# A recommender tower in 32 blocks per tile: other places for the parts, the portions and the last tile's MLP

## The reference

```python
e = stack([tbl_f[ids[:, f]] for f in range(32)], axis=1)        # (1024, 32, 64)
p, q = e[:, ROW_IDX], e[:, COL_IDX]                             # i and j of each of 496 pairs
z = einsum('bne,hne,bnh->bn', p, kernel, q)                     # kernel: (64, 496, 64)
h = concatenate([z, dense_ctx], axis=1)                         # (1024, 512)
h = maximum(h @ W_top1 + b_top1, 0)
h = maximum(h @ W_top2 + b_top2, 0)
y = h @ W_top3
```

## Time and profile before

| | |
|---|---|
| median of 3 runs | 755.47 us |
| the profiled execution | 754.49 us |
| its span, first to last instruction | 752.7 us |
| TensorE matmuls busy | 437.4 us, 58% of the span |
| VectorE busy | 361.6 us, 48% |
| ScalarE busy | 340.9 us, 45% |
| GpSimd busy | 241.9 us, 32% |
| granted TensorE clock, mean | 0.853 of 2.4 GHz |

### The profile page before, as it was taken

How to read it: one execution, slowest core, us unless ns; L and a number is a source line. 1 busy time by engine, 2 the same in 40 slices (tenths; PEclk the granted TensorE clock), 3 DMA queues, 4 the chain that set the end, 5 groups by cost and what they waited for, 6 DMA issues and landing times.

```text
span 752.7 us, 15352 instructions
## 1 busy us (share of the span) xinstructions
PE 437.4 (58%) x5552; PEld 320.8 (43%) x5552; DVE 361.6 (48%) x476; ACT 340.9 (45%) x2897; POOL 241.9 (32%) x260
## 2 busy tenths in 40 slices
PE   1001002588219971399614995159941599999896
PEld 1001001465007750168402783027820478777685
DVE  0010010697007870088601885028940388989881
ACT  0110000485226852267412774128641385986872
POOL 6777773003750047400573006720077100000000
PEclk9999999699559995599855998559975699999999
DMA  4663110000100001000010001100011000000000
GB/s 119 217 201 108 26 27 16 1 3 13 26 19 2 2 17 26 16 1 3 19 26 13 2 3 22 26 9 2 3 24 27 6 2 2 3 2 3 2 4 1
DMA packets 14571, 19.65 MB, mean 26 GB/s; under 512 B 7192, under 2 KB 7840, under 8 KB 14496
## 3 DMA queue, kind: packets, MB, share of 16 engines
q0 software_dynamic: 8192, 8.40, 5.6%
q1 hardware_dynamic: 6304, 10.27, 4.3%
HBM read 18.65 MB, written 0.00 MB: 25 GB/s over the span
## 4 chain that ended last, share of the span: by engine, by line
PE 42%; issue 36%; DVE 10%; ACT 5%; another core or an unknown queue 5%; POOL 1%; DMA 1%; DVEq 0%
PE side_ps L468 13%; PE u_ps L448 12%; PE u_ps L455 10%; DVE prod_s L383 6%; ACT prod_s L293 5%; PE side_ps L498 4%; DVE h L393 1%; DVE emb_t L357 1%; DVE prod_t L370 1%; POOL emb L252 1%; PE u_ps L433 1%; PE side_ps L514 1%; ACT h_t L320 1%; PE side_ps L490 1%
## 5 line engine op out<-in xcount | busy, mean ns | idle before, releaser
L293 ACT ACTIVATE prod_s<-prod_s 128x64 f32<-128x64 f32 x1408 | 300.2, 320 | 318.2 <-DVE prod_s L383 189.0
L252 POOL DMA_INDIRECT emb<-tbl,ids_sb x256 | 241.7, 944 | 344.2 <-DVE prod_s L383 265.7
L293 ACT ACTIVATION_READ_ACCUMULATOR prod_s<-prod_s 128x1 f32 x1408 | 267.7, 233 | 81.9 <-issue 81.8
L370 DVE TENSOR_TENSOR prod_t<-u_ps,emb_t 128x1024 f32<-128x1024 f32 x128 | 155.8, 1217 | 254.7 <-PE u_ps L448 211.7
L383 DVE TENSOR_TENSOR prod_s<-u_ps,emb 128x640 f32<-128x640 f32 (+4 forms) x192 | 158.4, 860 | 86.0 <-remote 40.5
L455 PE MATMUL u_ps<-k_sb,emb_t 64*128 64x512 f32 (+4 forms) x768 | 147.0, 495 | 88.0 <-issue 62.5
L468 PE MATMUL side_ps<-prod_t,pick_sb 128*32 128x128 f32 x2048 | 103.0, 284 | 162.4 <-issue 161.4
L448 PE MATMUL u_ps<-emb_t,k_sb 64*128 64x128 f32 x2048 | 146.8, 287 | 41.0 <-issue 34.1
L448 PEld LDWEIGHTS u_ps<-emb_t,k_sb 64*128 64x128 f32 x2048 | 134.1, 196 | 77.0 <-issue 54.4
L468 PEld LDWEIGHTS side_ps<-prod_t,pick_sb 128*32 128x32 f32 x2048 | 67.2, 112 | 194.5 <-issue 191.2
L455 PEld LDWEIGHTS u_ps<-k_sb,emb_t 64*128 64x128 f32 x768 | 62.8, 198 | 110.3 <-issue 71.4
(11 more groups left out here) (12 smaller groups left out, 22.6 us busy)
## 6 DMA issues: line engine op xcount, KB each, us to landing
k_sb<-k_pairs SPq DMA_DIRECT2D x16, 512.0 KB
emb<-tbl,ids_sb POOLq DMA_INDIRECT x256
w_sb<-w SPq DMA_DIRECT2D x1, 1024.0 KB
w_sb<-w SPq DMA_DIRECT2D x1, 512.0 KB
h<-dense SPq DMA_DIRECT2D x8, 8.0 KB
out<-y_row SPq DMA_DIRECT2D x8, 0.5 KB
ids_sb<-ids SPq DMA_DIRECT2D x1, 112.0 KB, 2.4
id_sb<-ident SPq DMA_DIRECT2D x1, 64.0 KB, 2.4
```

The source lines that it names most:

```text
L252: nc.gpsimd.indirect_dma_start(emb[t % EMBS][:, f * EMBED:(f + 1) * EMBED], None, tables[f], bass.IndirectOffsetOnAxis(ap=ids_sb[:, t, f:f ...
L293: last = nc.scalar.activation(slot, slot, ACT.Copy, accum_out=acc_ps[:, t % 2, column:column + 1])
L370: last = nc.vector.tensor_tensor(prod_t[at % TRING][:].rearrange("p (h x) -> p h x", h=HALVES), u, low.unsqueeze(1).to_broadcast([P, HALVE ...
```

## The change

Five things. (1) In the last group of blocks the ragged block y moves from the end to place 28, and the kinds of the blocks 26 to 31 go from T S T T T S to S T S T T T; numbers of each kind stay. (2) Parts 1 and 2 are turned behind blocks 5 and 13. (3) The portions stand behind blocks 5, 9, 13, 18, 23, 27 and 31. Where a portion and a part share a block, the portion comes first, as it did in the code before. (4) In the last tile, the third portion of picks stays behind block 29. (5) The last tile's rest is rewritten. The first layer's units go to the slots of blocks 29 and 30, the second's to that of block 31, one bank for each group of 128 units, with chunk 0 of the inputs first, before the last picks are there; the straight sums are transposed into the unused half of `acc_ps`; the relus alternate between ScalarE and VectorE, each with a semaphore. Elsewhere only names change (`last` becomes `done` or `stop`).

```diff
-    order = ["SS", "TSSTSS", "TSTTSTSTSS", "TSTTSTSTTSTTTS"]
+    order = ["SS", "TSSTSS", "TSTTSTSTSS", "TSTTSTSTSTSTTT"]
...
-        blocks += zip([*fulls[:2 * a], x, *fulls[2 * a:], y], [kind == "T" for kind in order[a]], strict=True)
+        group = [*fulls[:2 * a], x, *fulls[2 * a:], y]
+        if a == GROUPS - 1:
+            group = [*fulls[:2 * a], x, *fulls[2 * a:3 * a], y, *fulls[3 * a:]]
+        blocks += zip(group, [kind == "T" for kind in order[a]], strict=True)
...
-TURN_AT = {6: 1, 15: 2}
+TURN_AT = {5: 1, 13: 2}
...
-LATE_SPREAD_AT, HIDDEN1_AT, LATE_HIDDEN1_AT, HIDDEN2_AT, SUMS_AT, LATE_SUMS_AT, SPREAD_AT = 4, 8, 12, 17, 21, 25, 29
+LATE_SPREAD_AT, HIDDEN1_AT, LATE_HIDDEN1_AT, HIDDEN2_AT, SUMS_AT, LATE_SUMS_AT, SPREAD_AT = 5, 9, 13, 18, 23, 27, 31
+LAST_SPREAD_AT = 29
...
+        last = TILES - 1
+        h1_ps = [u_ps[SLOT_USE["u", last, n] % USLOTS][:, half * BANK:half * BANK + P]
+                 for n in (NB - 3, NB - 2) for half in range(2)]
+        h2_ps = [u_ps[SLOT_USE["u", last, NB - 1] % USLOTS][:, half * BANK:half * BANK + P] for half in range(2)]
+        spread_ps = acc_ps[:, (last + 1) % 2].rearrange("p (c b) -> p c b", c=S_CHUNKS)
...
# ScalarE
-            copy_acc(TILES - 1)
-            copy_spread(TILES - 1)
-            hidden1(TILES - 1)
-            hidden2(TILES - 1)
-            copy_logit(TILES - 1)
+            copy_acc(last)
+            act.wait_ge(last_turned, 1)
+            nc.scalar.activation(h0_t[:, T_CHUNKS:], spread_ps, ACT.Copy).then_inc(last_copied, 1)
+            act.wait_ge(picked, TILES * NT)
+            nc.scalar.activation(h0_t[:, 1], side_ps[:, 0], ACT.Copy).then_inc(last_copied, 1)
+            for m in (0, 2):
+                act.wait_ge(last_h1_mm, m + 1)
+                nc.scalar.activation(h1_t[:, m], h1_ps[m], ACT.Relu, bias=b1_sb[:, m:m + 1]).then_inc(last_h1_a, 1)
+            act.wait_ge(last_h2_mm, 1)
+            nc.scalar.activation(h2_t[:, 0], h2_ps[0], ACT.Relu, bias=b2_sb[:, 0:1]).then_inc(last_h2_a, 1)
+            copy_logit(last)
...
# VectorE
+            dve.wait_ge(weights_loaded, 80)
+            for m in (1, 3):
+                dve.wait_ge(last_h1_mm, m + 1)
+                nc.vector.tensor_scalar(h1_t[:, m], h1_ps[m], b1_sb[:, m:m + 1], 0.0, ALU.add, ALU.max,
+                                        ).then_inc(last_h1_v, 1)
+            dve.wait_ge(last_h2_mm, 2)
+            nc.vector.tensor_scalar(h2_t[:, 1], h2_ps[1], b2_sb[:, 1:2], 0.0, ALU.add, ALU.max).then_inc(last_h2_v, 1)
...
# TensorE
+            def last_hidden1(c, units, n):
+                pe.wait_ge(slot_emptied, used(last, n))
+                for m in units:
+                    done = nc.tensor.matmul(h1_ps[m], w1_sb[:, c, m * P:(m + 1) * P], h0_t[:, c],
+                                            start=(c == 0), stop=(c == 1))
+                    if c == 1:
+                        done.then_inc(last_h1_mm, 1)
+
+            def last_hidden2():
+                pe.wait_ge(slot_emptied, used(last, NB - 1))
+                for c in range(4):
+                    if c % 2 == 0:
+                        pe.wait_ge(last_h1_a, c // 2 + 1)
+                    else:
+                        pe.wait_ge(last_h1_v, c // 2 + 1)
+                    for m in range(2):
+                        done = nc.tensor.matmul(h2_ps[m], w2_sb[:, c, m * P:(m + 1) * P], h1_t[:, c],
+                                                start=(c == 0), stop=(c == 3))
+                        if c == 3:
+                            done.then_inc(last_h2_mm, 1)
...
-                    if n == SPREAD_AT:
+                    if n == (SPREAD_AT if t + 1 < TILES else LAST_SPREAD_AT):
                         spread(t)
-            late_spread(TILES - 1)
-            hidden1(TILES - 1, 0)
-            hidden1(TILES - 1, 1)
-            hidden2(TILES - 1)
-            logit(TILES - 1)
+            last_hidden1(0, range(2), NB - 3)
+            pick_sums(last, 1, 1, range(PORTION - 1))
+            last_hidden1(0, range(2, 4), NB - 2)
+            spread_straight(last, spread_ps).then_inc(last_turned, 1)
+            pick_sums(last, 1, 1, range(PORTION - 1, PORTION))
+            pe.wait_ge(last_copied, 1)
+            for c in range(T_CHUNKS, CHUNKS):
+                last_hidden1(c, range(4), NB - 2)
+            pe.wait_ge(last_copied, 2)
+            last_hidden1(1, range(4), NB - 2)
+            last_hidden2()
+            pe.wait_ge(last_h2_a, 1)
+            pe.wait_ge(last_h2_v, 1)
+            logit_sums().then_inc(logit_mm, 1)
```

More of the change, by code:

```diff
@@ L292, in sum_block @@
                     column = ACT_COLUMN[n] + at
-                    last = nc.scalar.activation(slot, slot, ACT.Copy, accum_out=acc_ps[:, t % 2, column:column + 1])
-                last.then_inc(summed_a, 1)
+                    done = nc.scalar.activation(slot, slot, ACT.Copy, accum_out=acc_ps[:, t % 2, column:column + 1])
+                done.then_inc(summed_a, 1)
             def copy_acc(t):
@@ L420, in turn_part @@
                 if t == 0:
-                    first, last = FIRST_PARTS[part]
-                    pe.wait_ge(first_gathered[part], 16 * 2 * (last - first))
+                    first, stop = FIRST_PARTS[part]
+                    pe.wait_ge(first_gathered[part], 16 * 2 * (stop - first))
                 else:
-                    first, last = PARTS[part]
+                    first, stop = PARTS[part]
                     fills = t // EMBS if t % EMBS == 0 else t // EMBS + 1
-                    pe.wait_ge(gathered[t % EMBS][part], 16 * 2 * (last - first) * fills)
+                    pe.wait_ge(gathered[t % EMBS][part], 16 * 2 * (stop - first) * fills)
                 u = slot_free(SLOT_USE["turn", t, part])
-                for m in range(first, last):
+                for m in range(first, stop):
                     for half in range(HALVES):
@@ L447, in block_u @@
                                 rows = slice(half * EMBED, (half + 1) * EMBED)
-                                last = nc.tensor.matmul(
+                                done = nc.tensor.matmul(
                                     u[:, half * BANK + d * P:half * BANK + (d + 1) * P],
@@ L458, in block_u, with pick_sums @@
                             k_sb[rows, n * BANK + s * EMBED:n * BANK + (s + w) * EMBED], start=True, stop=True)
-                last.then_inc(slot_filled, 1)
-            def pick_sums(t, chunk, portion):
-                for b in range(portion * PORTION, (portion + 1) * PORTION):
+                done.then_inc(slot_filled, 1)
+            def pick_sums(t, chunk, portion, some=range(PORTION)):
+                for b in range(portion * PORTION + some.start, portion * PORTION + some.stop):
                     at = t * NT + chunk * CHUNK + b
@@ L467, in pick_sums @@
                         _, quad, place = sum_place(b * HALVES * LOW + d)
-                        last = nc.tensor.matmul(side_ps[quad:quad + QUAD, 0],
+                        done = nc.tensor.matmul(side_ps[quad:quad + QUAD, 0],
                                                 pick_sb[:, 30 - 2 * place:62 - 2 * place],
@@ L471, in pick_sums @@
                                                 start=(place == 0), stop=(place == QUAD // 2 - 1))
-                    last.then_inc(picked, 1)
+                    done.then_inc(picked, 1)
             def sums(t):
@@ L497, in hidden1 @@
                     for c in range(4):
[L498 removed]
+                        done = nc.tensor.matmul(side_ps[:, m], w1_sb[:, c, m * P:(m + 1) * P], h0_t[:, c],
                                                 start=(c == 0), stop=(c == 3))
                 if portion == 1:
[L501 removed]
+                    done.then_inc(mlp_mm, 1)
             def hidden2(t):
```

40 lines of the change are left out of this document (25 added, 15 removed).

## The result

The changed kernel takes 721.14 us (719.99 to 722.05, 4 runs) where the kernel before takes 755.4 (752.46 to 755.55, 4 runs): a ratio of 0.9555, with an interval of 0.9528 to 0.9581. 729 was forecast, 8 too many.

What follows compares the result with a forecast made beforehand. TensorE and VectorE take turns waiting, neither full, with gather stalls in five of six stretches; 19.2 (six stretches at 3.2) + 2.3 + 5.15 = 26.6 us less, 727.9 profiled, so 729; range 722.5 to 736.5, chance 0.69.

Steps and rivals of the forecast that it cites:

- The walk of the two queues: Simulating TensorE and VectorE sharing three slots: a free tile falls from 50.1 to 46.9 us, 3.2 less.
- The work left is equal to some tenths.: Work remaining after a gather stall stays about equal, so each stall stretch gains 3.2 us too (bounds 1.5 to 5.1).
- Its signs of being wrong: Wrong if a stall stretch stays over 90.5 us or differs among tiles, or if ScalarE's sums release the products.
- No wait over 0.6: Expected sign in a free tile: no VectorE wait longer than 0.6 us.
- Rival 1: Gather stalls swallow the tile's gain; only free stretch and last tile gain, 10.7 us less, 744.8; chance 0.08.
- Last tile, up to its last product: In the last tile, block 3 to last product takes 44.9 us instead of 47.25, 2.3 less.
- Tail: From the last product to y: 13.80 us becomes 8.65, 5.15 less, with TensorE's clock at 2.4 GHz.
- rival 3: MLP at the end runs at half clock, taking 5.5 us more: 734.5; chance 0.07.
- Tile 0: The first tile, without an earlier tile's MLP and with few late waits, gains 0 us (bounds 0 to 1.5).
- Rival 2: VectorE becomes the bound entirely at 45.0 us per tile, 40 us less in all: 715; chance 0.05.
- Rival 4: Slower: each gather stall ends as late as tile 0's, 9.7 us more for five stalls, 48 in all: 777; chance 0.07.
- Rival 5: Waits in the tiles only change place; only the last tile gains, 7.5 us less: 748; chance 0.04.

Runs made afterwards that it cites:

- the paced kernel: Changed kernel with gather f of tiles 3 to 7 waiting for block f's product two tiles earlier: 622.35 us, ratio 0.8236 to the kernel before, stalling chip.
- the MLP alone: Kernel before with only the last tile's MLP rewritten, old order, parts and portions kept: 436.08 us, ratio 0.9906, free chip.

## Why the prediction was right, and where it was off

- **The walk of the two queues.** Right: 46.9 was said, 46.62 came. VectorE's waits were to sum to 1.93 and are 1.84, but in part by errors that cancel: block 10 0.35 said and 0.45 measured, part 2 0.17 and none, block 24 0.54 and 0.65, the early part 0.37 and 0.16, the next block 0 0.50 and 0.58. By the prediction's own sum 0.09 of the 0.3 us between 46.9 and 46.62 is waits and 0.24 VectorE's busy time, 44.76 and not 45.0. TensorE's wait at block 5 was walked as 0.59 and is 0.32 (the row at 621.38). (The prediction's list of VectorE's work adds up to 44.2 and not 44.3; nothing hangs on it.)
- **"The work left is equal to some tenths."** This is the step that was mis-sized. A stall stretch was to gain the 3.2 us of a free one, and gained 4.1, 4.5 us over five. I let part of block 5 go by before the slow pace and the rest in it, one matmul at a time. In fact all 16 of its matmuls, and eight picks behind them, went through in one go at 184.30, at full clock, after a gap of 1.52 us; only then came 20 picks in ones and twos, where there had been 22. So a block that I had half counted as work of the stall was done ahead of it. The stall's price fell by 0.6 us; the run with picks behind block 4 gives 0.3 of that back with the clock left out, and where the other 0.3 comes from is argued, not shown. Over five stretches 0.6 each is 3.1 us of the 4.5; the rest is the free tile's own 0.3 each. The 4.5 us are what put the time below the forecast's own range.
- **Its signs of being wrong.** Stall stretches were to be 88 to 89 us and not to differ among tiles. They are 86.78 to 88.20, so they do differ, by 1.4 us; that follows how long the clock stays at half behind the slow pace (the table above), which the prediction took as one fixed length, 3.9 us. "No wait over 0.6" was missed by the 0.65 at block 24. ScalarE's sums release no product, as was said.
- **Rival 1**, the stall taking the gain, asked for block 5 to pass the stall matmul by matmul, and for stretches that stay at 91.8 us. It passed as a burst.
- **Last tile, up to its last product**: 2.3 said, 2.26 measured.
- **Tail**: 8.65 said, 8.23 measured. From the last product at 0, the last of the first-layer instructions was to end at 5.0 and ends at 4.89, the second layer at 7.0 and 6.81, and the rest takes 1.42, not 1.65. The clock stayed at 1.00, so rival 3 was out. The reason given for it is not shown, though: the prediction laid the half clock of the tail before to the hole ahead of the first layer, and the same hole, in the kernel before without its late gathers on a free chip, left the clock at 1.00. So whether the change earned the 1.4 us of clock in the tail, or the one trace of before was unlucky there, isn't shown. TensorE's longest gap there is 0.54 us, at the relu that VectorE makes. The Trainium skill, "TensorE: Matmul & The Clock Gate", Part 1, has steady work release the clock; the trace agrees, with 1.00 from 579.70 to the end.
- **Tile 0** gained 0.6 and not 0, within its bounds of 0 to 1.5. The run with the old order begins tile 1's block 3 another 0.6 earlier than the changed kernel on its chip, so none of it is the order's.
- **Rival 2** needed VectorE at 45.0 per tile; it has 1.84 of waits left. **Rival 4**, a longer recovery from the gathers, did not happen: gathers start at 178.75 and the last at 217.4, and the slow pace ends at 223.7, 45.0 us after the first, as before. (The prediction's 5.3 us of recovery counts from the last gather's end at 219.4, not from its start, as it says.) **Rival 5** fell with the free tile.
- What the prediction did not ask is what the gathers' stall costs at all: some 315 us of 755, by the same kernel's 440 on the other kind. It took the 40 us as given, which was enough to price this change.

**Open.** What a gather takes from the other engines on a stalling chip, and why only there, wasn't found. One candidate is that the loading of instructions queues behind the gathers; in the trace of before, from 181 to 225 us, the DMA view has 1024 packets of the gathers' queue and none of the two instruction queues, which neither shows nor excludes it. Taking gathers out was not tried on a stalling chip, nor were the portions' places alone.

## What to carry to other kernels

Where two in-order queues share a few slots, walk both forward with durations from the trace, and check the walk on the kernel that you have: it gave every wait here to some tenths. Price a stall in instructions too: where an engine gets about a fixed number of them through, let them be those that carry most of the work. A mean over the stretches, and a second trace, are needed before 0.6 us can be read from stretches that differ by 1.4. And before polishing 3 us of a tile, ask what the 40 us beside it are: spreading gathers over the tile, one added wait, gave on a stalling chip four times what this change gave, and cost nothing on a free one.

## What the runs showed of the hardware

- In some runs, indirect gathers issued by GpSimd hold back the issue of TensorE and ScalarE: 22 matmuls and 45 ScalarE instructions in 40.1 us, most behind an "issue" gap. VectorE's long pause behind block 4, 37.96 us, is a wait for TensorE. 32 gathers take 45.0 us from the first to the end of the slow pace, and the 96 at the start 134.4 us: 1.40 us for each either way. They are issued 1.25 us apart, so work that takes 1.40 would form a backlog. The backlog itself stands in no view, but the rows of five in the paced kernel end 7.03 and 7.06 us after their first gather, as it would have them. In the free runs the same gathers, issued at the same 1.25 us, run beside a TensorE that loses nothing. The two queue rows, of the kernel before on a stalling chip (span 752.7 us) and of the MLP alone on a free one (434.7 us), say that the transfers themselves are no slower: 5.6% of 752.7 and 9.8% of 434.7 are both 42 us of the 16 engines.

```profile
q0 software_dynamic: 8192, 8.40, 5.6%
```

```profile
q0 software_dynamic: 8192, 8.40, 9.8%
```

- The Trainium skill, "SBUF — State Buffer", "Who interferes with whom", says of SBUF's ports that a DMA never contends with a compute engine, and that TensorE and ScalarE never wait on anyone. The free chip agrees (46.66 us a tile beside 35 us of GpSimd). On the stalling one both engines do lose time beside gathers, and no run shows whether it is lost at the ports, which is what the section is about: 20 of TensorE's matmuls one or two at a time behind up to 2.43 us of "issue" each, and 8.53 us of work in 39.41.
- The clock comes back late and unevenly: it was still 0.50 for 2.6 to 6.2 us after the slow pace had ended, with TensorE busy all the while, and a stretch's length follows it. The hole of 3.6 us ahead of the old MLP was followed by clock 0.50 in the trace of before and by 1.00 in that of the kernel without late gathers.
- The price hangs on the gathers' spacing, not on their number alone. The same 256 gathers cost the kernel before 315 us in bursts, and the changed one some 170 with a wait for a block ahead of each (582 us against 411 on a free chip).
